# Moving half of the normalising diagonals from GpSimd to VectorE, and all zero blocks to the start, in a causal attention layer

## What is computed

```
q = (x @ q_w.T + q_b).reshape(b, s, 16, 128);  k = x @ k_w.T + k_b;  v = x @ v_w.T + v_b
scores = einsum('bqhd,bkd->bhqk', q, k) / sqrt(128), causal
attn = softmax(scores);  out = einsum('bhqk,bkd->bqhd', attn, v)
x = layernorm(x + out @ o_w.T + o_b)
x = layernorm(x + x @ (weight * scale_weight[:, None]).T + bias)
```

## Time and profile before

| | |
|---|---|
| time, median of 3 runs | 2328.3 us (2321.86, 2328.3, 2329.09) |
| the profiled execution's own time | 2322.83 us |
| its span, slowest core | 2321.3 us (core 5; the others 2306.6 to 2319.5 us) |
| VectorE busy | 891.2 us (38%) |
| ScalarE busy | 842.5 us (36%) |
| TensorE busy, matmuls | 1552.3 us (67%) |
| GpSimd busy | 489.0 us (21%) |
| attention | from about 361 us to about 1530 us |

### The profile page before, as it was taken

How to read it: one execution, slowest core, us unless ns; L and a number is a source line. 1 busy time by engine, 2 the same in 40 slices (tenths; PEclk the granted TensorE clock), 3 DMA queues, 4 the chain that set the end, 5 groups by cost and what they waited for, 6 DMA issues and landing times.

```text
span 2321.3 us, 26657 instructions; the slowest of 8 cores (2306.6 to 2321.3 us)
## 1 busy us (share of the span) xinstructions
PE 1552.3 (67%) x7216; PEld 671.7 (29%) x7216; DVE 891.2 (38%) x1921; ACT 842.5 (36%) x2078; POOL 489.0 (21%) x591
## 2 busy tenths in 40 slices
PE   0899954555655666665666666686968778778682
PEld 0344422322222222222233333332323223223230
DVE  0000003445555555555555555510525422326324
ACT  0122113544444555554554455432234121224321
POOL 0000012321111111111000000023435343445331
PEclk9999976667666677676667677798979898898886
DMA  9222299800000000000000000034523436442352
GB/s 147 37 45 37 37 109 109 101 1 1 1 1 1 1 1 1 1 1 1 1 1 1 1 1 1 1 104 127 155 86 109 145 120 188 134 139 91 89 156 83
DMA packets 43644, 137.11 MB, mean 59 GB/s; under 512 B 5835, under 2 KB 5868, under 8 KB 42988
## 3 DMA queue, kind: packets, MB, share of 16 engines
q1 hardware_dynamic: 28988, 84.02, 11.4%
q0 software_dynamic: 5296, 34.60, 11.4%
q10 hardware_dynamic: 9216, 16.78, 2.7%
HBM read 153.21 MB, written 33.55 MB: 80 GB/s over the span
## 4 chain that ended last, share of the span: by engine, by line
PE 38%; issue 16%; DVE 15%; DMA 13%; ACT 10%; POOL 3%; another core or an unknown queue 3%; DVEq 1%; ACTq 0%; SPq 0%; POOLq 0%
PE psT L259 10%; ACT expS L406 8%; DMA xres<-xT 8%; DVE mpart L385 8%; PE psO L491 7%; PE psT L843 5%; POOL ycs L804 3%; PE psS L348 3%; DMA outT<-outb 2%; PE psO L843 2%; PE psU L843 2%; PE psS L449 2%; DVE expST L468 2%; DMA trib_s<-tri 2%
## 5 line engine op out<-in xcount | busy, mean ns | idle before, releaser
L427 POOL TENSOR_SCALAR diagP<-ident_s,rcp 128x128 bf16<-128x128 bf16 x256 | 154.1, 602 | 1039.0 <-DVE rcp L423 692.5
L406 ACT ACTIVATE expS<-psS,negm 128x512 bf16<-128x512 f32 (+3 forms) x367 | 225.4, 620 | 358.1 <-DVE negm L389 287.7
L491 PE MATMUL psO<-expST,Vsb 128*128 128x512 bf16 x640 | 253.7, 541 | 69.2 <-ACT expST L473 42.5
L449 PE MATMUL psS<-diagP,expS 128*128 128x128 bf16 x1250 | 153.5, 268 | 140.1 <-ACT expS L406 117.9
L259 PE MATMUL psT<-xTbf,qwst 128*128 128x512 bf16 x1024 | 221.2, 379 | 0.2 <-ACT Vsb L241 0.2
L348 PE MATMUL psS<-KT,QTO 128*128 128x512 bf16 (+3 forms) x367 | 164.7, 489 | 73.8 <-ACT expS L406 48.1
L418 DVE TENSOR_REDUCE den<-dpart 128x1 f32<-128x2 f32 (+2 forms) x192 | 29.9, 156 | 428.9 <-ACT expS L406 394.5
L385 DVE TENSOR_REDUCE mpart<-psS 128x1 f32<-128x512 f32 (+3 forms) x329 | 187.6, 611 | 3.6 <-PE psS L348 3.6
L406 ACT ACTIVATE expS<-psT,negm 128x512 bf16<-128x512 f32 (+3 forms) x179 | 111.0, 624 | 166.4 <-DVE negm L389 152.7
L449 PEld LDWEIGHTS psS<-diagP,expS 128*128 128x128 bf16 x1250 | 107.0, 121 | 190.5 <-issue 184.7
L376 DVE TENSOR_REDUCE negm<-psS 128x1 f32<-128x256 f32 (+3 forms) x38 | 18.5, 488 | 361.3 <-PE psS L357 361.3
(11 more groups left out here) (94 smaller groups left out, 2387.4 us busy)
## 6 DMA issues: line engine op xcount, KB each, us to landing
wost<-wo_bf SPq DMA_DIRECT2D x64, 512.0 KB, 3.9
fwst<-fw_bf SPq DMA_DIRECT2D x64, 512.0 KB, 3.9
xres<-xT ACTq DMA_DIRECT2D x64, 256.0 KB, 3.9
outT<-outb SPq DMA_DIRECT2D x64, 256.0 KB, 3.7
xTbf<-xT POOLq DMA_DIRECT2D x1, 8192.0 KB, 59.7
qwst<-qw POOLq DMA_DIRECT2D x16, 512.0 KB, 5.6
wo_bf<-wo POOLq DMA_DIRECT2D x4, 2048.0 KB, 80.7
fw_bf<-fw POOLq DMA_DIRECT2D x4, 2048.0 KB, 99.4
```

The source lines that it names most:

```text
L406: e.activation(expS8[:, (par * 4 + qt % 4) * S + kc * W: (par * 4 + qt % 4) * S + kc * W + wdt], slot[:, 0:wdt], AF.Exp, bias=negm8[:, nco ...
L427: ncol=ncol: e.tensor_scalar(diagP[:, (par * 4 + j) * 128:(par * 4 + j + 1) * 128], ident_s[:], rcp8[:, ncol:ncol + 1], None, AluOpType.mult),
L449: qt=qt: e.matmul(bk[:, i * 128:(i + 1) * 128], expS8[:, (par * 4 + qt % 4) * S + kt * 128: (par * 4 + qt % 4) * S + (kt + 1) * 128], diag ...
L491: base=base: e.matmul(bk[:, 0:W], Vsb[:, kt * 128:(kt + 1) * 128], expST2[:, base + kt * W: base + (kt + 1) * W], start=(kt == 0), stop=(k ...
```

## The change

The diagonal of query tiles j = 1 and j = 3 is made by VectorE instead of GpSimd, by the same operation; j = 0 and 2 stay on GpSimd. Its event is then one of counter `v`. The 48 zero blocks of all four chunks are cleared before the first chunk, 24 for each half of `expST2`, instead of 12 at the beginning of each chunk.

```diff
-                E_diag2v[par][j] = p.op("gpsimd", lambda e, par=par, j=j,
+                deng = "gpsimd" if j % 2 == 0 else "vector"
+                E_diag2v[par][j] = p.op(deng, lambda e, par=par, j=j,
                                         ncol=ncol: e.tensor_scalar(
                     diagP[:, (par * 4 + j) * 128:(par * 4 + j + 1) * 128],
                     ident_s[:], rcp8[:, ncol:ncol + 1], None,
                     AluOpType.mult),
-                    waits=[E_rq, E_trmm2[par][j]], inc="p")
+                    waits=[E_rq, E_trmm2[par][j]],
+                    inc="p" if j % 2 == 0 else "v")
...
-            for c in range(NCH):
-                for sl in range(2):
-                    ev = None
-                    for kt in range(4 * c + 1, 4 * c + 4):
-                        for jj in range(kt - 4 * c):
+            for sl in range(2):
+                ev = None
+                for cc in range(NCH):
+                    for kt in range(4 * cc + 1, 4 * cc + 4):
+                        for jj in range(kt - 4 * cc):
                             ev = p.op("gpsimd", lambda e, sl=sl, kt=kt,
                                       jj=jj: e.memset(
...
                                 waits=[E_Q_all], inc="p")
-                    E_msd[sl] = ev
+                E_msd[sl] = ev
+            for c in range(NCH):
                 for step in range(H + 2):
```

## The result

The changed kernel took 2356.1 us (median of 8 runs, 2354.06 to 2363.98), the kernel before 2326.0 us (8 runs): a ratio of 1.0135, 95% interval 1.0121 to 1.0149, that is 28 to 35 us more. The prediction was 2352 us, range 2333 to 2368. The profiled execution took 2348.8 us, 26.0 more than that of before; the sum for it was 2350. Every ratio in this document compares only executions in which neither half of the eight cores ran at a visibly lower clock than the other.

The account below looks back on a forecast made before the run. The prediction took VectorE and ScalarE working by turns to bound the attention. Its terms, +41 - 12 - 1.5 = +27 us, on 2322.8 us gave 2350 us, stated as 2352 us; 8-in-10 range 2333 to 2368 us.

Parts of the forecast that it names:

- A circle of VectorE and ScalarE bounds the attention: Attention: the two engines work by turns; an instruction added to VectorE between `rcp` and `negm` is paid in full.
- 128 moved diagonals: VectorE, behind `rcp` in odd units: each delays the next instruction by 0.32 us, +41 us (33 to 49).
- Dropped waits: Waits for the diagonal's event two heads later, and `negm`'s own wait in chunk 0, go: together -12 us.
- The part hidden: Chunk 0's waits for TensorE and the chunk ends hide some of the addition: -1.5 us (0 to -3).
- seven waits for TensorE in chunk 0: Before the maximum in seven units of chunk 0, 0.35 to 0.6 us each, hiding part of the addition.
- The faster chunk ends: At each chunk's end the last diagonal (j = 3), wanted at once, would be there some 0.5 us sooner.
- ScalarE's waits some 35 us longer: Changed profile: ScalarE's waits before the exponentials grow by some 35 us in all.
- Zero blocks free: 48 blocks at the start take 7.2 us within TensorE's wait for the triangle; clearing early gains at most 1 us.
- The wait for `rcp` is free: Rival, VectorE: a diagonal costs only its 0.16 us slot; +7 us in all, 2330 to 2335 us; chance 0.06.
- TensorE sets the pace: Rival, attention: late score pieces absorb VectorE's addition; no change, 2323 to 2328 us; chance 0.05.
- much slower: Rival, VectorE diagonals: reading the factor for each partition adds 0.2 us each, +53 us, about 2376 us; chance 0.05.
- The starting point: Whole kernel: +27 us on the profiled execution's 2322.8 us gives 2350; that execution is 5.5 us below the three-run median.

Follow-up runs that it names:

- e2: Kernel before with only the diagonals of j = 1 and 3 moved to VectorE, zero blocks left where they were: ratio 1.0123 to the kernel before.
- e3: Changed kernel with all 256 diagonals on VectorE: ratio 1.0281 to the kernel before.
- e5: Changed kernel with VectorE's 128 diagonals emitted behind the `negm` of the next unit: ratio 0.9943 to the kernel before.
- e6: Kernel before with `den`, `rcp` and the diagonal of a unit emitted behind the next unit's `negm`: 1979 us, ratio 0.8527.
- e4: Kernel before without the waits for the diagonal of two heads ago in chunk 0's exponentials, `den` and `rcp`: ratio 0.9908.
- e1: Changed kernel with all diagonals back on GpSimd, so only the zero blocks are moved: ratio 1.0007 to the kernel before.
- e8: Kernel before with the odd diagonals on VectorE, each behind the copy that follows `rcp`: ratio 1.0045 to the kernel before.
- e9: e6 without the waits for the diagonal of two heads ago: 1975 us, ratio 0.8508 to the kernel before.
- e7: e6 with the odd diagonals on VectorE: ratio 0.8514 to the kernel before.
- e10: e7 without the waits for the diagonal of two heads ago: ratio 0.8517 to the kernel before.

## Why the prediction was right, point by point

- **A circle of VectorE and ScalarE bounds the attention, and GpSimd's diagonal lies beside it**: shown by the nearly full price between `rcp` and `negm` (e2, e3), by none behind `negm` (e5), and by e6.
- **128 moved diagonals, +41 us (33 to 49)**: measured 0.27 us from `rcp` to the diagonal in 111 and 0.28 us in 17 of 128, then 0.16 to 0.18 us to the next instruction in 127 of 128, so 0.27 + 0.17 - 0.10 = 0.34 us each, 43.5 us. The duration was 0.255 us, not 0.22 us, and the overlap with the next instruction 0.08 us, not 0.06 us. The size was 2.5 us off.
- **By the Trainium skill ("VectorE: DVE Perf Modes", the perf-mode tiers) the estimate was 0.18 us**: the trace has 0.255 us, nearer to the plain 0.29 us of a copy. Whether the four-element mode was on can't be told from it.
- **Dropped waits, -12 us**: the gaps are 0.09 to 0.11 us in 95 of the odd `den` after, and in chunk 0 `negm` starts 0.10 us behind `rcp` in heads 2 and later too. e4 shows the 0.07 us and 0.05 us by themselves at twice the count: -20 us expected, -21 us found; e5 adds that it stays when the diagonal's cost goes: -12 us expected, -13 us found.
- **The part hidden, -1.5 us (0 to -3)**: 43.5 - 12.1 = 31.4 us stand against 28.3 us between the reciprocals, so some 3 us are hidden or scatter. Of the seven waits for TensorE in chunk 0 the view still marks two (0.21 and 0.36 us); in nine units `negm` starts 0.14 or 0.15 us behind the end of the copy, where it starts 0.08 us ahead of it when nothing holds it up, so the rest of these waits went into short gaps. Chunk 0 grew by 4.2 us against 5.6 us by the terms, so 1.4 us were hidden there, about as assumed. The faster chunk ends are not seen: from the last reciprocal of a chunk to the first of the next it is 7.9, 9.1 and 12.6 us before, 7.5, 9.5 and 12.9 us after.
- **ScalarE's waits some 35 us longer**: too high. They grew by 25 us in chunks 1 to 3 and not at all in chunk 0 (78.9 + 10.8 us before, 89.2 us after). The 96 odd units of chunks 1 to 3 at 0.34 us, less the 0.07 us that `den` starts sooner, give 26 us; the prediction gives no working for its 35, and both terms were known to it.
- **Zero blocks free**: shown by e1, in the span between the reciprocals to within about 1 us. The prediction did not see that blocks left at a chunk's beginning can hold a diagonal on VectorE up (e2); the size, 0.5 us, lies within its "at most 1 us".
- **The wait for `rcp` is free** (rival, from the section on the drain in "VectorE: DVE Perf Modes" of the Trainium skill): false here. 0.27 us against 0.10 us in the trace, and e8, which moves only the place, gets back 0.8% of the kernel between the 1.0123 of e2 and its own 1.0045 (18 us; 128 x 0.17 = 22 us was expected). Between the reciprocals the median core gets back 21.5 us (1186.3 to 1164.8 us).
- **TensorE sets the pace; much slower**: neither came. VectorE waited for score matmuls in a handful of places, as before, and the factor read for each partition added at most the 0.035 us by which the duration was missed.
- **The starting point**: the sum for the profiled execution was 2350 us, and it took 2348.8. That it comes so close is in part luck: the attention took 28.3 us more where +27 was forecast, and the first reciprocal came 1.1 us earlier and the rest behind the last one was 1.4 us shorter, which neither edit accounts for. The median of before turned out at 2326.0, on which the sum of +27 gives 2353; 2356.1 were measured.

## What to carry to other kernels

Before moving an instruction to an engine with idle time, look at what ends that idle time: where two engines work by turns, both look half idle, and every instruction and every satisfied wait between the one's last result and the other's next start is paid nearly in full. The same instruction was free here a few places further on, behind the result that the other engine waits for. And where the views show such turns, the work to do is to reorder so that one unit's end isn't awaited before the next one's begin: that gave 15% here, where balancing the engines lost 1.3%.

## What the runs showed of the hardware

- A wait that has long been satisfied costs about 0.07 us on VectorE and 0.05 us on ScalarE if the engine has nothing else to do meanwhile (`den` 0.17 against 0.10 us behind the row sum), and nothing that can be seen behind a copy (in chunk 0 `negm` starts 0.08 or 0.09 us ahead of the copy's end with its old wait, before, and without it, e5) or in an order with slack (e9 against e6, within some 5 us). 248 on VectorE and 56 on ScalarE were worth 21 us.
- A VectorE instruction that waits for a predecessor of 0.16 us starts 0.25 to 0.28 us after that one's start (`rcp` behind `den` in 189 of 192 units before, the diagonal behind `rcp` in all 128 after); one that need not wait starts 0.10 us after it (`rcp` and the copy behind it).
- A diagonal on VectorE that began while GpSimd cleared blocks did not end before GpSimd had finished them. In the profiled cores of e2, e7, e8 and e10 this met 7 diagonals, which lasted 0.37 to 1.44 us instead of about 0.25 us and ended 0.04 to 0.05 us behind the last block. No run varies the operation to show which kinds are held up so.
- TensorE's mean granted clock in the attention was 0.69 when it stood idle between the turns, and 0.87 when nearly the same matmuls came closer together (e6): 693 us of them in 1120 us against 540 us in 780 us.
